# Turning y for the feed-forward part: transposing transfers of 16-bit halves in place of TensorE's turns

## The reference, cut to what matters

```python
x = x + attn(cond(x, itok_B_0_15, ...), ...)
y = einsum('bsi,boi->bso', x, weight[itok_B_3_7])        # 512 -> 512, matrix by batch
logits = y @ gate_w;  routing, _ = top_k(logits, 2)
h      = relu(y @ up_w) ** 2                              # 512 -> 1024
shared = h @ down_w                                       # 1024 -> 512
routed = ((y @ fc1_w) @ expert_w * sum(routing)) @ fc2_w
out    = x + layernorm(shared + routed) * gamma + beta
```

## Time and profile before

| | |
|---|---|
| median of three runs | 1165.48 us |
| profiled execution, its time | 1163.74 us |
| profiled execution, its span | 1162.0 us |
| around the span | 1.74 us |
| TensorE busy (share of the span) | 1127.1 us (97%) |
| GpSimd, VectorE, ScalarE busy | 61%, 57%, 48% |
| share of the chain that ended last: TensorE | 93% |
| mean granted TensorE clock | 0.991 |

### The profile page before, as it was taken

One profiled execution on the slowest core, in us unless ns is written; L12 is line 12 of the kernel. 1 busy time (PEld: TensorE's weight loads), 2 busy tenths in 40 slices (PEclk: granted clock), 3 DMA queues, 4 the chain that ended last, 5 costly groups with the idle time before them and its releaser, 6 DMA issues.

```text
span 1162.0 us, 27444 instructions
## 1 busy us (share of the span) xinstructions
PE 1127.1 (97%) x11124; PEld 898.3 (77%) x11124; DVE 657.0 (57%) x1042; ACT 552.3 (48%) x915; POOL 708.4 (61%) x610
## 2 busy tenths in 40 slices
PE   6999999999999999999999999999999999999994
PEld 4777787878777878787777688787878788787883
DVE  5767666666666666666665264464545455453432
ACT  4466767676767676656576323323141423322120
POOL 3456787878787878787765454456455454433332
PEclk9999999999999999999998999999999999999997
DMA  6135645565555554445356832222413122020100
GB/s 259 40 100 170 202 160 196 160 199 163 195 163 195 167 191 151 155 129 186 103 181 214 302 128 90 82 92 74 139 46 131 55 90 92 28 82 28 46 28 36
DMA packets 60203, 152.38 MB, mean 131 GB/s; under 512 B 11312, under 2 KB 12080, under 8 KB 54704
## 3 DMA queue, kind: packets, MB, share of 16 engines
q1 hardware_dynamic: 42432, 105.83, 27.2%
q0 software_dynamic: 12224, 34.10, 9.3%
q10 hardware_dynamic: 5424, 10.71, 2.6%
HBM read 98.16 MB, written 38.27 MB: 117 GB/s over the span
## 4 chain that ended last, share of the span: by engine, by line
PE 93%; DVE 2%; issue 2%; DMA 1%; POOL 1%; ACT 0%; SPq 0%; DVEq 0%; ACTq 0%
PE bank L565 22%; PE pair L756 15%; PE bank L732 15%; PE bank L656 9%; PE bank L607 8%; PE bank L749 8%; PE pair L630 3%; PE bank L555 3%; PE pair L583 3%; PE bank L615 2%; PE bank L642 2%; PE bank L703 1%; PE bank L595 1%; PE bank L693 1%; DMA x_rows<-x1t 1%
## 5 line engine op out<-in xcount | busy, mean ns | idle before, releaser
L1549 POOL TENSOR_TENSOR w_lo<-w2t,w_hi 128x2048 fp32r<-128x2048 f32 x38 | 175.6, 4621 | 7.1 <-ACT w_hi L915 7.0
L565 PE MATMUL bank<-wqkv_hi,h_hi 128*128 128x512 f32 x384 | 158.7, 413 | 0.5 <-issue 0.2
L1603 POOL TENSOR_TENSOR u_lo<-act,u_hi 128x512 fp32r<-128x512 f32 x64 | 82.6, 1291 | 115.7 <-ACT u_hi L1093 115.6
L565 PE MATMUL bank<-wqkv_hi,h_lo 128*128 128x512 f32 x384 | 150.6, 392 | 0.0
L565 PE MATMUL bank<-wqkv_lo,h_hi 128*128 128x512 f32 x384 | 149.7, 390 | 0.0
L732 PE MATMUL bank<-yT_hi,up_hi 128*128 128x512 f32 x256 | 103.4, 404 | 0.7 <-DVE yT_lo L1247 0.7
L1406 DVE TENSOR_TENSOR act<-act 128x512 f32<-128x512 f32 x59 | 48.8, 827 | 95.5 <-ACT act L1089 95.5
L756 PE MATMUL pair<-down_hi,u_hi 128*128 128x512 f32 x256 | 100.9, 394 | 0.0
L756 PE MATMUL pair<-down_hi,u_lo 128*128 128x512 f32 x256 | 100.8, 394 | 0.0
L732 PE MATMUL bank<-yT_hi,up_lo 128*128 128x512 f32 x256 | 100.6, 393 | 0.0
L756 PE MATMUL pair<-down_lo,u_hi 128*128 128x512 f32 x256 | 100.3, 392 | 0.0
(11 more groups left out here) (178 smaller groups left out, 2930.3 us busy)
## 6 DMA issues: line engine op xcount, KB each, us to landing
w2t<-in_w SPq DMA_DIRECT2D x38, 1024.0 KB
vx<-v_hl SPq DMA_DIRECT2D x128, 68.0 KB
x_rows<-x1t SPq DMA_DIRECT2D x32, 256.0 KB
x1g<-x_rows SPq DMA_DIRECT2D x32, 256.0 KB, 2.7
kx<-k_hl SPq DMA_DIRECT2D x124, 64.0 KB
yt<-y_rows SPq DMA_DIRECT2D x7, 1024.0 KB, 6.3
ffn_high<-w_high SPq DMA_DIRECT2D x20, 256.0 KB
ffn_low<-w_low SPq DMA_DIRECT2D x20, 256.0 KB
```

The source lines that it names most:

```text
L565: m = e.matmul(into, a[:, c, :], b[:, n, c, :], start=(c == 0 and k == 0), stop=(c == KC - 1 and k == 2))
L1549: e.tensor_tensor(w2_lo[:, :, :], w2t[:, :, :], w2_hi[:, :, :].bitcast(F32), ALU.subtract).then_inc(d_wlo, 1)
L1603: e.tensor_tensor(u_lo[n % FC][:, :], act[n % 2][:, :], u_hi[n % FC][:, :].bitcast(F32), ALU.subtract) \
```

## The change

- `ys` and `y_rows` hold each 32-bit word of y as two 16-bit halves, apart: a row is 512 low halves and then 512 high halves (1024 of 16 bits, as many bytes as before). `slot_out` becomes two copies on ScalarE, each reading every second 16-bit element of the bank.
- `load_y` becomes eight transposing transfers for a group, each 512 tokens by 128 half-words: one for each chunk and half. They land as [128 features, 512 tokens] in `yt`. `f_y` counts 128 per group. For group 1 they stand in SyncE's order behind `store_x1(29)`, before they stood ahead of `spread_v(31)`.
- `join_y(m, c)`: two copies, each of 512 half-words into every second half-word of a 128x512 tile of words, which lies in place of `yT_lo` (for group 0 in the place of a tile of the up weights). For groups 1 to 7 ScalarE does them ahead of `high_y`; for group 0 VectorE does all eight in iteration 31, ahead of `add_x(27)`.
- `high_y` and `low_y` read these words from SBUF. `turn` and its 128 transposes on TensorE are gone, with the waits in them; two of these move to `gate_products` and `turn_gates`.

```diff
-    ys = [sb(f"ys{i}", [P, DM]) for i in range(2)]
+    early_route = overlaid("early_route", [P, 2, DM])
+    ys = [sb(f"ys{i}", [P, 2, DM], U16) for i in range(2)]
...
-    yt = sb("yt", [P, GROUP, DM])
-    yT_hi, yT_lo = [sb("yT_hi0", [P, KC, TOK], F32R)], [sb("yT_lo0", [P, KC, TOK], F32R)]
+    yt = sb("yt", [P, KC, 2, TOK], U16)
+    yT_hi = [sb("yT_hi0", [P, KC, TOK], F32R)]
+    y_words = [overlaid("y_words0", [P, KC, TOK])]
+    yT_lo = [sb("yT_lo0", [P, KC, TOK], F32R)]
...
+    def words(m, c):
+        return y_words[m % 2][:, c, :] if m else words_first[:, UP_CHUNKS // KC * c + 1, :]
+    def halves(word, n):
+        return word.bitcast(U16)[:, n::2]
...
-                    e.wait_ge(S["t"], KC * m)
+                    e.wait_ge(S["word"], KC * m)
...
-                e.dma_start(rows_of(m)[:, :, :], y_rows[rows, :].rearrange("(t p) n -> p t n", p=P)).then_inc(f_y, 16)
+                for c in range(KC):
+                    for n in range(2):
+                        cols = slice(DM * n + P * c, DM * n + P * c + P)
+                        e.dma_start(rows_of(m)[:, c, n, :], y_rows[rows, cols], transpose=True) \
+                            .then_inc(f_y, 16)
...
-            load_y(1)
             spread_v(T - 1)
             store_x1(T - 3)
+            load_y(1)
...
-            def turn(m, c):
...
-                for t in range(GROUP):
-                    k = e.transpose(turned(m, c)[:, P * t:P * t + P], rows_of(m)[:, t, P * c:P * c + P], ident)
-                k.then_inc(S["t"], 1)
...
-                e.activation(ys[s % 2][:, :], bank_, ACT.Copy).then_inc(d_mc, 1)
+                for n in range(2):
+                    k = e.activation(ys[s % 2][:, n, :], halves(bank_, n), ACT.Copy)
+                k.then_inc(d_mc, 1)
...
+            def join_y(m, c):
+                if c == 0:
+                    e.wait_ge(f_y, 2 * KC * 16 * (m + 1))
...
+                for n in range(2):
+                    k = e.activation(halves(words(m, c), n), rows_of(m)[:, c, n, :], ACT.Copy)
+                k.then_inc(S["word"], 1)
+            def high_y(m, c):
+                e.wait_ge(S["word"], KC * m + c + 1)
+                e.activation(yT_hi[m % 2][:, c, :], words(m, c), ACT.Copy).then_inc(S["hi"], 1)
...
                     relu(n)
                     if ahead:
                         for c in turns(m, f):
+                            join_y(m + 1, c)
                             high_y(m + 1, c)
...
-                e.tensor_tensor(yT_lo[m % 2][:, c, :], turned(m, c), yT_hi[m % 2][:, c, :].bitcast(F32),
+                e.tensor_tensor(yT_lo[m % 2][:, c, :], words(m, c), yT_hi[m % 2][:, c, :].bitcast(F32),
                                 ALU.subtract).then_inc(S["lo"], 1)
...
+                if i == T - 1:
+                    e.wait_ge(f_y, 2 * KC * 16)
+                    for c in range(KC):
+                        join_y(c)
                 if live(i - 4):
                     add_x(i - 4)
```

More of the change, by code:

```diff
@@ L33 @@
 I32 = mybir.dt.int32
+U16 = mybir.dt.uint16
 ALU = mybir.AluOpType
@@ L121, in program @@
     x1_rows = nc.dram_tensor("x1_rows", [TOKENS, DM], F32, kind="Internal").ap()
-    y_rows = nc.dram_tensor("y_rows", [TOKENS, DM], F32, kind="Internal").ap()
+    y_rows = nc.dram_tensor("y_rows", [TOKENS, 2 * DM], U16, kind="Internal").ap()
     route_rows = nc.dram_tensor("route_rows", [P, KC, DM], F32, kind="Internal").ap()
@@ L132, in program, with overlaid @@
     sb = tiles_in(top)
+    def overlaid(name, shape, dt=F32):
+        with ExitStack() as stack:
+            return tiles_in(stack)(name, shape, dt)
     def psum(name, shape, dt=F32):
@@ L266, in u_tiles @@
                 {"u_hi": u_hi, "u_lo": u_lo}[n][f] = sb(f"{n}{f}", [P, TOK], F32R)
+    words_first = overlaid("words_first", [P, UP_CHUNKS, DM])
     up_hi = sb("up_hi", [P, UP_CHUNKS, DM], F32R)
@@ L278, in program @@
     yT_hi.append(sb("yT_hi1", [P, KC, TOK], F32R))
+    y_words.append(overlaid("y_words1", [P, KC, TOK]))
     yT_lo.append(sb("yT_lo1", [P, KC, TOK], F32R))
@@ L297, in program @@
     first_y = ExitStack()
-    yt_first = tiles_in(first_y)("yt_first", [P, GROUP, DM])
+    yt_first = tiles_in(first_y)("yt_first", [P, KC, 2, TOK], U16)
     first_y.close()
@@ L312, in program @@
     lnw = cst[:, C_BIAS:C_IDENT].rearrange("p (a n) -> p a n", a=2)
-    route_f = [ys[0], ys[1], total[0], total[1]]
+    route_f = [early_route[:, 0, :], early_route[:, 1, :], total[0], total[1]]
     s_cst, s_ids, s_masks, s_qkln = sem("s_cst"), sem("s_ids"), sem("s_masks"), sem("s_qkln")
@@ L361, in program @@
     f_out = [sem(f"f_out{i}") for i in range(2)]
-    fn = ("t", "hi", "lo", "g", "gc", "gt", "gtc", "log", "best", "w", "u", "relu", "act", "uhi", "ulo", "rp", "dr", "route",
+    fn = ("word", "hi", "lo", "g", "gc", "gt", "gtc", "log", "best", "w", "u", "relu", "act", "uhi", "ulo", "rp", "dr", "route",
           "tot", "bn", "aggr", "eps", "rstd", "gam", "bet", "res")
     S = {n: sem(f"f_{n}_") for n in fn}
-    def turned(m, c):
-        return (B4, B5)[c % 2] if m else (B4, B6, B5, B3)[c]
+    def words(m, c):
+        return y_words[m % 2][:, c, :] if m else words_first[:, UP_CHUNKS // KC * c + 1, :]
+    def halves(word, n):
+        return word.bitcast(U16)[:, n::2]
     def rows_of(m):
@@ L699, in gate_products @@
                 e.wait_ge(m_glo, 1)
+                if m:
+                    e.wait_ge(S["gc"], m)
                 for c in range(KC):
@@ L708, in turn_gates @@
                 e.wait_ge(S["gc"], m + 1)
+                if m:
+                    e.wait_ge(S["gtc"], m)
                 for t in range(GROUP):
@@ L830, in _ @@
             turn_qk(T - 1, kn[(T - 1) % 2], "kn", B2, "tk")
-            upto(e, "olo", T - 5)
-            turn(0, 0)
             turn_qk(T - 1, qn[(T - 1) % 2], "qn", B7, "tq")
[L834 to L841, removed]
             values(T - 4, 0)
@@ L845, in _ @@
             scores(T - 2, 1)
-            e.wait_ge(S["lo"], 1)
             turn_values(T - 4)
@@ L881, in _ @@
                         turn_slot(slot_up(m), B6)
-                    if ahead:
-                        for c in turns(m, f):
-                            turn(m + 1, c)
                     if f == slot_at(m)[1] and slot_up(m) < SLOTS:
@@ L940, in fetch_up @@
                     .then_inc(ready, 16)
-            def high_y(m, c):
-                e.wait_ge(S["t"], KC * m + c + 1)
+            def join_y(m, c):
+                if c == 0:
+                    e.wait_ge(f_y, 2 * KC * 16 * (m + 1))
                 if m >= 2 and c == 0:
@@ L948, in high_y @@
                     upto(e, "r", T - 1)
-                e.activation(yT_hi[m % 2][:, c, :], turned(m, c), ACT.Copy).then_inc(S["hi"], 1)
+                for n in range(2):
[4 more added lines that the diff above has]
+                e.activation(yT_hi[m % 2][:, c, :], words(m, c), ACT.Copy).then_inc(S["hi"], 1)
             def gates_out(m):
@@ L1111, in _ @@
             high_probs(T - 3)
+            e.wait_ge(S["lo"], KC)
             fetch_up(m_up[1], 0, 1, 8)
@@ L1243, in add_x, with join_y @@
                 e.tensor_tensor(x1t[t % 2][:, :], B6, xt[t % XR][:, :], ALU.add).then_inc(A["x1"], 1)
+            def join_y(c):
+                for n in range(2):
+                    k = e.tensor_copy(halves(words(0, c), n), rows_of(0)[:, c, n, :])
+                k.then_inc(S["word"], 1)
             def low_y(m, c):
                 e.wait_ge(S["hi"], KC * m + c + 1)
-                e.tensor_tensor(yT_lo[m % 2][:, c, :], turned(m, c), yT_hi[m % 2][:, c, :].bitcast(F32),
+                e.tensor_tensor(yT_lo[m % 2][:, c, :], words(m, c), yT_hi[m % 2][:, c, :].bitcast(F32),
                                 ALU.subtract).then_inc(S["lo"], 1)
@@ L1513, in scatter_slot @@
                 e.wait_ge(d_mc, s + 1)
-                e.indirect_dma_start(out=y_rows, out_offset=rows(slot_rows, s), in_=ys[s % 2][:, :],
+                e.indirect_dma_start(out=y_rows, out_offset=rows(slot_rows, s), in_=ys[s % 2][:, :, :].rearrange("p a n -> p (a n)"),
                                      in_offset=None, bounds_check=TOKENS - 1,
```

## The result

| | before, beside it | after |
|---|---|---|
| median of four runs | 1164.81 us | 1181.56 us |
| profiled execution, its span | 1162.0 us | 1181.7 us |
| mean granted TensorE clock | 0.991 | 0.978 |

The ratio is 1.0146, with a 95% interval of 1.0122 to 1.0171: slower by 1.5%, about 17 us. The predicted 1161.2 us said slightly faster. The range of 1157 to 1190 holds the time, but only by the rivals that it reached out to. The two profiled executions lie 19.7 us of span apart, some 3 us more than the medians: before's took 1163.74 us, 1.1 under its median, and the changed kernel's 1183.52, 2.0 over.

A forecast was written before the change was run, and what follows sets the result against it. TensorE's own work was taken as the bound; -10.5 + 2.0 + 1.7 + 1.5 + 1.0 = -4.3 us on the profiled 1163.74 gave 1159.4, and 1161.2 us as median. Range 1157 to 1190 with rivals, 1157 to 1164 without.

The forecast's parts named there:

- 24 turns off the chain: Groups 1 to 6: removing four transposes of 0.44 us per chunk from TensorE's chain saves 10.5 us.
- iteration 28: Main loop, load for group 0: the next spread of k follows 12.6 us later, so no cost was charged.
- `low_y(0, 0)` and the transition: Transition, VectorE: reading two SBUF tiles beside GpSimd's subtraction ends about 1.5 us later; +1.5 us (bounds 0 and 2.1).
- store of x1: Group 0: the moved megabyte shares the DMA engines with this store; +1.0 us (bounds 0 and 2.6).
- four copies behind `up(0, 7)`: Group 0, ScalarE: joins of chunks 2 and 3 delay `gate_products(1)`; +2.0 us (bounds 1.4 and 3.3).
- clock behind these: After TensorE's gap ahead of `gate_products(1)`: granted clock falls to 0.50; +1.7 us (0 if the clock stays).
- T and its covers: Eight transfers, first issue to last landing: 8.2 us; covers 21 us (groups 1-6), 12.6 (iteration 28), 11.8 (group 0).
- The second rival: Group 0: transfers taking 12 to 21 us delay the store of x1; 1164 to 1169 us, chance 0.20.
- The third rival: Groups and group 0: transfers from 21 us on become the bound; up to some 1225 us, chance 0.20.
- the fourth: Groups 1 to 6: ScalarE becomes the bound at 0.83 us a join copy; 1171 us, chance 0.08.
- The copy theory: Theory tested in the experiments, whole kernel: added copies on ScalarE and VectorE cost the time; 1180 to 1182 with plain pieces.

## Why the prediction was wrong

Term by term, from the two profiled executions. Each row names an instruction that both have, with its start in before and after; what earlier rows already explain is taken off:

| term | predicted | measured | read from |
|---|---|---|---|
| 24 turns off the chain | -10.5 | -11.4 | 6 x (65.62 - 63.72) |
| iteration 28 | 0 | +9.7 | next weight load, 562.08 to 571.82 |
| `low_y(0, 0)` and the transition | +1.5 | +1.5 | `up(0, 0)`, 613.01 to 624.28, less 9.7 |
| store of x1 | +1.0 | +11.6 | its landing, 654.76 to 677.65, less 11.3 |
| clock behind that store | none | +2.9 | `relu(7)`, 662.84 to 688.61, less 22.9 |
| four copies behind `up(0, 7)` | +2.0 | +2.7 | gate products, 665.42 to 693.86, less 25.8 |
| clock behind these | +1.7 | +2.7 | the end, +19.7, less 28.4 - 11.4 |
| sum | -4.3 | +19.7 | |

The last row is what is left over. Read directly, `up(1, 0)` starts 31.19 us later (704.31 and 735.50), which is 2.75 more than the gate products.

**The failed step is T and its covers.** T, the time from the first issue to the last landing, was sized from a plain row, the spread of k: 0.69 us for each of four transfers, so 8.2 us. For plain transfers that was near: with plain pieces of 256 bytes in iteration 28 it is about 8.6 us (an estimate: the last leaves at 543.1, 4.5 behind the first, and the median landing is 4.1). A transposing one is dearer to issue, and in the crowd much dearer. The DMA issues of three stretches, iteration 28, group 0 and group 1 (last figure: median us to landing), answer to the earlier trace rows:

```profile
yt_first<-y_rows SPq DMA_TRANSPOSE x8, 3.9
...
yt<-y_rows SPq DMA_TRANSPOSE x8, 10.9
...
yt<-y_rows SPq DMA_TRANSPOSE x8, 3.6
```

In iteration 28 and in the groups, eight issue in 10.37 to 11.63 us, and with the landing of the last T is about 14 (an estimate from 11.43, less one issue, plus 3.9). In group 0, beside the fetches of other weights, issuing alone took 21.17, and T was 27.5 us: ScalarE's wait for y, above, ends at 675.04, and the first issue was at 647.49. So T lay in the bounds of 6.3 to 28.4, in group 0 near the upper one, and the row taken was near the lower one.

**Two covers were missed.** For iteration 28 the prediction looked at the next spread of k, 12.6 us behind the load. The weights of slot 23 stand 5 us behind it, and ScalarE waits for them with the softmax queued behind. The exchange of the two orders shows the cause (9.2 us back for a measured 9.7). In group 0 the prediction looked at the store alone. Group 1's y has a reader of its own there, ScalarE's first join: the relu ahead of it ends at 663.73, 16.2 us behind the first issue, and T of 27.5 passed that by the 11.3 us of the wait.

**The second rival had the right place in group 0 and too small a price.** It took the store as late by T - 11.8, and stopped at T = 21. In the changed kernel what holds the store is the issuing and not the landing: at 21.2 the formula gives 9.4 us, at 27.5 it would give 15.7. The store left 10.7 us late and took 7.85 us for 6.96, so it landed 11.6 us late. That rival did not see the clock behind the wait, the late y beside the store, nor iteration 28, and so stopped at 1169 us. The cause there is more than the queue: plain pieces of 256 bytes leave the queue in 8.52 us and still delay the store (15.29 us), 1 KB pieces don't. The windows (last three figures: clock, DMA share, GB/s) of the plain pieces of 256 bytes, of those of 1 KB and of the changed kernel:

```profile
642.00:657.00 15.00, 15.00 (x73) 11.26 (x71) 3.63 (x11) 3.80 (x7) 6.99 (x3) 1.00 1.05 335
...
642.00:657.00 15.00, 15.00 (x73) 11.40 (x72) 4.24 (x12) 6.59 (x12) 6.98 (x3) 1.00 1.01 363
...
647.00:669.00 22.00, 18.46 (x178) 13.97 (x176) 5.43 (x15) 7.80 (x11) 9.32 (x5) 1.00 0.97 272
```

The engines are full in all three, and they move less in the smaller pieces, least with the transposing transfers. The Trainium skill says as much in "DMA: Bandwidth & Descriptors", section "Why small descriptors are slow (HBM only)", by a fixed cost for each packet; the trace agrees in direction (335 for 363 GB/s).

**The third rival did not come in groups 1 to 6.** Loads 2 to 7 had their 21 us of cover and needed about 14: no wait of TensorE is seen behind 705 us. Its sign, ScalarE's join waiting for y, showed in group 0 alone. Nor did the fourth: a join copy took 772 ns, more than the 0.6 taken and below the bound of 0.83, yet TensorE waits for no relu in the groups. **The copy theory falls** but for the place behind `up(0, 7)`, where the copies cost 2.7 us and a clock drop of 2.7, both foreseen and both undone by joining the chunks earlier (6.7 us measured). That `low_y(0, 0)` would stall beside GpSimd was right (2.03 us for 0.68). It ends 0.55 us behind GpSimd's subtraction; in the earlier trace rows it was 0.54 behind as well, and not at the same time, as the prediction read it:

```profile
617.79 1.90 POOL L1557 TENSOR_TENSOR probs<-probs,row_max 128x1024 f32<-128x1024 f32 x1 [2.58 <-DVE row_max L1217]
...
618.21 2.03 DVE L1257 TENSOR_TENSOR yT_lo<-words_first,yT_hi 128x512 fp32r<-128x512 f32 x1
```

That the table's +1.5 equals the forecast is luck, though. Of it, `low_y` is worth 1.0 us: it starts 10.27 us later than in before (607.94 and 618.21), and `up(0, 0)` 11.27. The other half microsecond was there already, for the statistics ahead of the joins come 9.72 us later (597.85 and 607.57). It comes from VectorE's eight joins, which were forecast as hidden: beside them an addition of GpSimd took 2.66 us for 0.24 (shown at the end), and the layer norm behind it came late.

Of the two rules of the Trainium skill weighed beforehand neither gives the time here. By "Advanced Engine Details and Errata", section on the X-bar transpose, such transfers are as fast as regular ones: eight took about 14 us in iteration 28, for about 8.6 with plain pieces of the same size. By the other page, "VectorE: DVE Perf Modes", section "The three transpose paths", 32 blocks in a row would be an estimated 41.9 us: they were done in about 14, and in 27.5 in the crowd.

**Left open.** What makes one transposing transfer take 1.2 us to issue, and one in the crowd 6.53, was not taken apart. No run with group 1's transfers in this place kept y in time and only the store late, or the other way round, so the two waits of ScalarE in group 0 are not separated. With the joins moved, the gate products start 1.5 us ahead of before's (663.96 for 665.42) though the first `up` starts 2.5 us behind (615.53 for 613.01). Part of it is seen: TensorE stands 0.38 us ahead of them, in before 1.74, and the eight transposes of group 1 that before had there are gone. The rest was not taken apart.

## What to carry to other kernels

Before a transfer is replaced by several, list everything behind it in the issuing engine's queue, down to the loads for other parts of the program, and ask who waits for each and what stands behind the waiting instruction. Look beside the chain for a second wait that ends just before the one it shows. Price new transfers in the busiest stretch in which they are issued, and by the size of their pieces. A change that gains in the steady part and loses at two places of the transition may only want other places: here 1181.56 us became 1151.23, 1.2% below the kernel before, by moving issues and copies alone.

## What was not expected of the hardware

- Issuing a transposing transfer of 512x128 half-words took SyncE 1.26 us in the median (1.14 at the least), and up to 6.53 us in the crowd of group 0; the plain load of a whole megabyte took 0.37 to 0.52. The Trainium skill, "DMA: Bandwidth & Descriptors", section "Issuing engines are not separate DMA queues", calls issue time usually small beside the transfer; here issuing takes 11.43 of the 14 us from the first issue to the last landing.
- The same strided copy of 128x512 half-words took ScalarE 772 ns (two in a row 1.28 us on the chain) and VectorE 456 ns (eight in a row 2.79 us). VectorE's copies held up GpSimd's addition of 128x2 elements beside them: it took 2.66 us, and 0.24 when they were moved away. The two in the changed kernel, and the addition in before:

```profile
607.74 2.79 DVE L1252 COPY words_first<-yt_first 128x512 uint16<-128x512 uint16 x8
...
607.91 2.66 POOL L1594 TENSOR_SCALAR var_eps<-mean_var 128x2 f32<-128x2 f32 x1 [0.41 <-DVE mean_var L1401]
...
598.19 0.24 POOL L1580 TENSOR_SCALAR var_eps<-mean_var 128x2 f32<-128x2 f32 x1 [0.41 <-DVE mean_var L1391]
```
